# A four-layer attention and feed-forward network on one core: the query and key columns of three attentions are put in another order in memory

## The reference, cut to what matters

```python
q = _heads(x @ Wq + bq)            # (b, 16 heads, 512, 16)
k = _heads(src @ Wk + bk)          # src is x (causal) or the context
v = _heads(src @ Wv + bv)
att = jnp.einsum('bhqd,bhkd->bhqk', q, k) * scale
y = jnp.einsum('bhqk,bhkd->bhqd', jax.nn.softmax(att, axis=-1), v)
y = y.transpose(0, 2, 1, 3).reshape(x.shape[0], T, C)
return y @ Wp + bp
```

## Time and profile before

| What | Value |
|---|---|
| median of 3 runs | 3605.73 us |
| lowest and highest run | 3598.47, 3623.86 us |
| the profiled execution's own time | 3604.23 us |
| its span in the profile | 3602.4 us |
| PE busy | 2886.6 us, 80% |
| DVE busy | 2034.1 us, 56% |
| ACT busy | 1460.1 us, 41% |
| POOL busy | 1147.6 us, 32% |
| DMA packets | 129751, 198.50 MB |

### The profile page before, as it was taken

One profiled execution on the slowest core, in us unless ns is written; L12 is line 12 of the kernel. 1 busy time (PEld: TensorE's weight loads), 2 busy tenths in 40 slices (PEclk: granted clock), 3 DMA queues, 4 the chain that ended last, 5 costly groups with the idle time before them and its releaser, 6 DMA issues. The chain is left out here.

```text
span 3602.4 us, 44895 instructions
## 1 busy us (share of the span) xinstructions
PE 2886.6 (80%) x16756; PEld 1623.2 (45%) x16756; DVE 2034.1 (56%) x3607; ACT 1460.1 (41%) x1932; POOL 1147.6 (32%) x1007
## 2 busy tenths in 40 slices
PE   5998898758867979999876889877899899688544
PEld 2333333533324534444662344356778778223222
DVE  4545546756635735444784666675453543566588
ACT  1444455415652224444422545432433432256522
POOL 2122222221322215555413668741001010122233
PEclk7688889878987989999986989988999999689766
DMA  6344454034521001111100000000221121555100
GB/s 158 76 100 96 103 117 102 19 73 93 112 61 37 1 21 37 37 40 61 60 7 12 1 1 1 13 12 11 68 72 56 56 65 35 114 109 106 29 15 15
DMA packets 129751, 198.50 MB, mean 55 GB/s; under 512 B 36288, under 2 KB 66496, under 8 KB 129408
## 3 DMA queue, kind: packets, MB, share of 16 engines
q1 hardware_dynamic: 97792, 143.23, 17.3%
q0 software_dynamic: 31744, 52.41, 5.3%
HBM read 130.73 MB, written 64.75 MB: 54 GB/s over the span
## 5 line engine op out<-in xcount | busy, mean ns | idle before, releaser
L2202 DVE TENSOR_REDUCE L_mx<-bank_t 128x2 f32<-128x1024 f32 (+3 forms) x512 | 562.5, 1121 | 481.0 <-PE bank_t L2010 300.9
L2409 ACT ACTIVATE L_P<-bank_t 128x1024 f32<-128x1024 f32 (+2 forms) x512 | 478.1, 945 | 483.8 <-PE bank_t L2024 305.8
L2202 DVE TENSOR_REDUCE L2a_mx<-bank_t 128x2 f32<-128x1024 f32 x256 | 311.4, 1222 | 406.7 <-PE bank_t L1987 406.1
L2409 ACT ACTIVATE L2a_P<-bank_t 128x1024 f32<-128x1024 f32 x256 | 261.6, 1023 | 289.4 <-PE bank_t L1999 289.1
L2024 PE MATMUL bank_t<-L_QS,L_KS 50*128 50x512 f32 (+2 forms) x1024 | 242.5, 477 | 111.6 <-DVE L_mx L2202 81.6
L2010 PE MATMUL bank_t<-L_KS,L_QS 48*128 48x512 f32 (+2 forms) x1024 | 262.0, 514 | 75.2 <-DMA L_QS<-L_spill_q_halves 64.5
L1987 PE MATMUL bank_t<-L2a_QK 32*128 32x512 f32 x1536 | 257.5, 453 | 69.9 <-DVE L2a_mx L2202 34.0
L2055 PE MATMUL bank_o<-L_P,L_V 128*32 128x512 f32 (+3 forms) x2048 | 289.8, 642 | 2.6 <-ACT xn L2416 1.8
L1995 PE MATMUL bank_t<-L2a_QK 32*128 32x512 f32 x1536 | 260.4, 448 | 0.0
L2010 PEld LDWEIGHTS bank_t<-L_KS,L_QS 48*128 48x128 f32 x1024 | 107.9, 209 | 320.5 <-issue 222.2
L1987 PEld LDWEIGHTS bank_t<-L2a_QK 32*128 32x128 f32 x1536 | 138.9, 199 | 234.3 <-issue 106.3
(11 more groups left out here) (432 smaller groups left out, 6059.8 us busy)
## 6 DMA issues: line engine op xcount, KB each, us to landing
L_KS<-L_spill_k_halves SPq DMA_DIRECT2D x174, 128.0 KB, 4.5
L_QS<-L_spill_q_halves SPq DMA_DIRECT2D x174, 128.0 KB, 4.9
L_spill_raw<-xn POOLq DMA_DIRECT2D x64, 256.0 KB, 2.5
L2g_raw<-in_L_ffn_h_blocks SPq DMA_DIRECT2D x32, 512.0 KB, 3.4
L_spill_k_halves<-L_hi SPq DMA_DIRECT2D x32, 256.0 KB, 2.1
L_spill_k_halves<-L_lo SPq DMA_DIRECT2D x32, 256.0 KB, 2.3
L_spill_q_halves<-L_hi SPq DMA_DIRECT2D x32, 256.0 KB, 4.8
L_spill_q_halves<-L_lo SPq DMA_DIRECT2D x32, 256.0 KB, 5.0
```

The costliest lines, as they stand in the source:

```text
L2202: e.tensor_reduce(neg, s.tile[:, :, 0:n_keys], AX.X, ALU.max, negate=True).then_inc(sem(s.done), 1)
L2409: e.activation(s.at.Pr[s.pb][:, :, q0:S], s.tile[:, :, q0:S], ACT.Exp, scale=s.at.scale).then_inc(sem(s.exp), 1)
```

## The change

The columns of `Wq` and `Wk` of the three attentions, and the entries of their biases, are put in another order on the host, before the kernel starts: within each 128 columns, from (slot, part, d) to (part, d, slot). A projected half then has row 64q + 4d + s for part q, column d of the head, slot s. The four slots that one partition of a stack takes are now four neighbouring rows of the stored half, 8 KB in one run. The rearrangement in ReadStack follows. The values' weights and the output's weights stay as they are. The loads of weights keep their shapes and their order.

```diff
@@ L0_xattn (L0_first, L1_weights and L3_xattn likewise)
-            loads = [weight_load(W[n][:, :, :], f"L0_xattn_{n}", KC) for n in W]
-            loads += [weight_load(Wc[n][:, :, :], f"L0_xattn_{n}", 1) for n in Wc]
+            loads = [weight_load(W["Wv"][:, :, :], "L0_xattn_Wv", KC), weight_load(W["Wcq"][:, :, :], "L0_xattn_Wcq_runs", KC)]
+            loads += [weight_load(Wc["Wck"][:, :, :], "L0_xattn_Wck_runs", 1), weight_load(Wc["Wcv"][:, :, :], "L0_xattn_Wcv", 1)]
...
@@ sync_program, ReadStack
                     for r, part in enumerate((0, 0, 1) if s.which == "q" else (0, 1, 0)):
-                        halves = s.spill[part].rearrange("(s q d) n -> q d s n", q=st.q_of, d=D)
+                        halves = s.spill[part].rearrange("(q d s) n -> q d s n", q=st.q_of, d=D)
                         for q in range(st.q_of):
                             row = st.part * q + D * r
                             e.dma_start(stack[row:row + D, s.slots, :].bitcast(F32),
...
@@ layout, on the host
+    for n in ("L0_xattn_Wq", "L0_xattn_Wk", "L0_xattn_Wcq", "L0_xattn_Wck", "L1_xattn_Wq", "L1_xattn_Wk",
+              "L3_xattn_Wq_T", "L3_xattn_Wk_T", "L0_xattn_bq", "L0_xattn_bk", "L0_xattn_bcq", "L0_xattn_bck",
+              "L1_xattn_bq", "L1_xattn_bk"):
+
+        w = a[n].reshape(-1, a[n].shape[-1] // P, 4, 2, 16)
+        a[n + "_runs"] = w.transpose(0, 1, 3, 4, 2).reshape(a[n].shape)
```

More of the change, by code:

```diff
@@ L933, in L0_first @@
             f.bq, f.bp = sb(scope, "L0_bcols", [P, 4, KC]), sb(scope, "L0_bp", [P, C])
-            f.loads = [weight_load(f.W["Wk"][:, :, :], "L0_xattn_Wk", KC), load(f.bq[:, 1, :], dram["L0_xattn_bk_cols"]),
-                       weight_load(f.W["Wq"][:, :, :], "L0_xattn_Wq", KC), load(f.bq[:, 0, :], dram["L0_xattn_bq_cols"])]
+            f.loads = [weight_load(f.W["Wk"][:, :, :], "L0_xattn_Wk_runs", KC), load(f.bq[:, 1, :], dram["L0_xattn_bk_runs_cols"]),
+                       weight_load(f.W["Wq"][:, :, :], "L0_xattn_Wq_runs", KC), load(f.bq[:, 0, :], dram["L0_xattn_bq_runs_cols"])]
             f.e_bp = row_load(f.bp, "L0_xattn_bp")
@@ L954, in L0_xattn @@
                 fetch_x(b)
-            loads = [weight_load(W[n][:, :, :], f"L0_xattn_{n}", KC) for n in W]
-            loads += [weight_load(Wc[n][:, :, :], f"L0_xattn_{n}", 1) for n in Wc]
+            loads = [weight_load(W["Wv"][:, :, :], "L0_xattn_Wv", KC), weight_load(W["Wcq"][:, :, :], "L0_xattn_Wcq_runs", KC)]
+            loads += [weight_load(Wc["Wck"][:, :, :], "L0_xattn_Wck_runs", 1), weight_load(Wc["Wcv"][:, :, :], "L0_xattn_Wcv", 1)]
             loads += [weight_load(Wo[:, :, :], "L0_xattn_Wp", KC)]
-            loads += [load(bq[:, i, :], dram[f"L0_xattn_{n}_cols"]) for i, n in ((2, "bcq"), (3, "bck"))]
+            loads += [load(bq[:, i, :], dram[f"L0_xattn_{n}_runs_cols"]) for i, n in ((2, "bcq"), (3, "bck"))]
             loads += [row_load(rows[n], f"L0_xattn_{n}") for n in rows]
@@ L1164, in fetch @@
             def fetch():
-                w.loads[:] = [weight_load(w.Wq[:, :, :], "L1_xattn_Wq", KC), weight_load(w.Wk[:, :, :], "L1_xattn_Wk", 1),
+                w.loads[:] = [weight_load(w.Wq[:, :, :], "L1_xattn_Wq_runs", KC), weight_load(w.Wk[:, :, :], "L1_xattn_Wk_runs", 1),
                            weight_load(w.Wv[:, :, :], "L1_xattn_Wv", 1), weight_load(w.Wo[:, :, :], "L1_xattn_Wo", KC),
-                           load(w.bq[:, 0, :], dram["L1_xattn_bq_cols"]), load(w.bq[:, 1, :], dram["L1_xattn_bk_cols"]),
+                           load(w.bq[:, 0, :], dram["L1_xattn_bq_runs_cols"]), load(w.bq[:, 1, :], dram["L1_xattn_bk_runs_cols"]),
                            row_load(w.bv, "L1_xattn_bv"), row_load(w.bo, "L1_xattn_bo")]
@@ L1629, in L3_xattn @@
             Wv = sb(scope, "L3_Wv", [P, 1, C])
-            loads = [weight_load(Wq[:, :, :], "L3_xattn_Wq_T", KC), weight_load(Wo[:, :, :], "L3_xattn_Wo_T", KC),
-                     weight_load(Wk[:, :, :], "L3_xattn_Wk_T", 1), weight_load(Wv[:, :, :], "L3_xattn_Wv_T", 1)]
+            loads = [weight_load(Wq[:, :, :], "L3_xattn_Wq_T_runs", KC), weight_load(Wo[:, :, :], "L3_xattn_Wo_T", KC),
+                     weight_load(Wk[:, :, :], "L3_xattn_Wk_T_runs", 1), weight_load(Wv[:, :, :], "L3_xattn_Wv_T", 1)]
             e_ctx = load_context(ahead["context"])
@@ L2673, in cols @@
             a[n + "_cols"] = a[n].reshape(-1, P).T
-    cols("L0_xattn_bq", "L0_xattn_bk", "L0_xattn_bcq", "L0_xattn_bck")
     def flip(*names):
@@ L2683, in layout @@
     a["L2_ffn_w3_blocks"] = a["L2_ffn_w3_w"].T.reshape(KF, P, KC, P)
-    cols("L0_ffn_b1", "L1_ffn_b1", "L1_xattn_bq", "L1_xattn_bk", *(f"L2_ffn_{n}_s" for n in ("w1", "w2", "h1", "h2")))
+    cols("L0_ffn_b1", "L1_ffn_b1", *(f"L2_ffn_{n}_s" for n in ("w1", "w2", "h1", "h2")))
     a["L3_xattn_Wk_T"], a["L3_xattn_Wv_T"] = a["L3_xattn_Wkv"][:C].T, a["L3_xattn_Wkv"][C:].T
+    for n in ("L0_xattn_Wq", "L0_xattn_Wk", "L0_xattn_Wcq", "L0_xattn_Wck", "L1_xattn_Wq", "L1_xattn_Wk",
[3 more added lines that the diff above has]
+        a[n + "_runs"] = w.transpose(0, 1, 3, 4, 2).reshape(a[n].shape)
+    cols(*(f"{n}_runs" for n in ("L0_xattn_bq", "L0_xattn_bk", "L0_xattn_bcq", "L0_xattn_bck", "L1_xattn_bq",
+                                 "L1_xattn_bk")))
     a["L1_ffn_scale"] = a["L1_ffn_scale"].reshape(1, 1)
```

## The result

| | before | after |
|---|---|---|
| median | 3604.64 us (20 runs, 3587.66 to 3627.01) | 3621.61 us (20 runs, 3608.41 to 3650.21) |
| ratio | | 1.0058, 95% interval 1.0039 to 1.0078 |
| span of the profiled execution | 3602.4 us | 3648.4 us |
| mean granted clock of that execution | 0.866 | 0.853 |

The changed kernel is slower, by 0.6%, or some 20 us. The interval of the ratio does not reach 1, so the forecast of a gain of 0 to 9 us was wrong in sign, though the median lies within the range of 3570 to 3630 us.

The account below looks back on a forecast made before the run. PE was taken as the first bound, DMA counting only where PE waits. Eight waits of two groups at 0.2 us, three at 0.3 us, and 0.3 us for maxima give 4.4 us off 3604.2, so 3600 us; range 3570 to 3630.

Parts of the forecast that it names:

- the forecast of a gain of 0 to 9 us: Main forecast for the whole kernel, centred on 3600 us, chance 0.63.
- The stake and the waits: PE's 14 waits for the query stack, 64.5 us; eleven within reach, 40.3 us; with the maxima's waits 88 us at stake.
- slot 0: Reads at an attention's start, three waits of 24.2 us in sum; keep 2 KB runs, priced at nothing.
- the five long ones: Five of the eleven waits for the query stack within reach, 28.7 us in sum.
- Packets and issue: Stack reads: 17,856 fewer packets of 129,751, bytes unchanged; SP's issue of six reads gains 0 us.
- Transfer: Moving a group of six stack reads, 5.7 us: longer packets save 3.5%, or 0.2 us per group.
- The faster one: Rival: the narrow DRAM source limits stack reads, spreading it raises the rate; 3575 us, at the bound 3567; chance 0.25.
- the 164 GB/s of the broadcast: Read of the inverse sums from 16 KB of DRAM into 128 partitions, taken as evidence for the faster rival.
- The slower one: Rival: with 8 KB packets engines change over less often, stack reads fall to 111 GB/s; 41 us more, 3645 us; chance 0.07.
- The rule of the Trainium skill: DMA rate goes with ports reached; partitions 0 to 15 reach four of 16, 104 GB/s; it speaks against the change.
- the group stays at 5.7 us: By the port rule alone, six stack reads take as long as before and the sum is zero.

Follow-up runs that it names:

- a unit's chain: Program of its own: six reads, a 512 KB store, its landing, six reads, their landing; 15.79 us in the old order, 16.50 in the new.
- reads alone: Programs with only rounds of six stack reads, everything else left out; 7.40 us a round in the old order, 7.92 in the changed kernel's.
- the new order in packets of 2 KB: Changed kernel with stored rows 2.5 KB apart instead of 2 KB, so packets are 2 KB again; ratio 1.0022 to the kernel before.
- the target spread: Stack reads into every third of 48 partitions, against the kernel before: old order 0.991, new order 0.9887, old order with the queries' store ahead 0.9912.
- the store ahead: Kernel before with the keys' reads issued one tick later, behind the store of the queries' halves; ratio 1.010.

## Why the prediction was wrong

*The stake and the waits* were read rightly. 14 waits, 11 of them within reach and slot 0 outside it: after the change nearly the same waits are there (15), those of slot 0 and the five long ones about the same in sum (23.5 and 28.5 us), most of the short ones longer, 67.6 us in all against 64.5.

*Packets and issue* came out to the number: 17,856 packets fewer, 2.7 us to issue six reads, nothing gained there.

*Transfer* is the step that failed. I took 36 ns of 1032 ns off a partition's 8 KB, 0.2 us per group, from the 12 ns of a packet that do not grow with its bytes. Measured, a group alone is 0.5 us longer (7.92 against 7.40 us), and a unit's chain of two groups 0.7 us longer. No run shows a price of the short packets that could be given back: from SBUF, 2 and 8 KB differ by 0.1 us in 9. And the new layout has a price, which I had not put into the sum at all. With reads alone it goes with the place: rows 10 KB apart instead of 2.5 cost 0.5 us per group with the same packets of 2 KB. I named the place once, for slot 0 ("rows 8 KB apart in DRAM"), and set it to nothing there; it is 0.13 us for its twelve reads. The same distance holds for all the other reads.

*Which property of the layout costs the time in the whole kernel stays open.* There the new order in packets of 2 KB had the old rate and the old landings (143 GB/s; 4.3 and 4.8 us) and ran 14 us faster than the changed kernel, which points to the runs of 8 KB; the reads alone point to the place. Runs of 8 KB cannot stand 2 KB apart, so the two cannot be parted in full, and no run tells why they come out differently. Shown is that the new layout as a whole makes a group slower.

*The rivals.* The faster one looked to the source, with the sign wrong: I read the 164 GB/s of the broadcast as "a narrow source is slow", when a source spread wider is what turned out slower. The slower one had the sign (a rate of 115 to 131 GB/s in place of 137) and its price, 41 us, was for 111 GB/s. Its cause, long packets into two narrow targets in turn, is not borne out by the reads alone, but it is not ruled out either: in the whole kernel the loss went when the packets were cut to 2 KB, and it was not seen with the target spread.

*The rule of the Trainium skill* that I weighed, "SBUF — State Buffer", section "Door 1: The DMA port swizzle (why [64,N] ≈ [32,N])", by which 16 neighbouring partitions are the limit, is borne out: every third of 48 partitions took a round from 7.27 to 6.19 us and the kernel down by 0.9%. The rule says nothing on a distance at the source, and "the group stays at 5.7 us" was what I drew from it; as long as the target is narrow, the layout at the source still adds to it.

*The size.* 7.7 us are worked out from the chains, 10 us are measured at an equal clock, 17 to 27 us in the medians. The remaining part goes with a granted clock that is 0.004 lower. The direction is the same in the other runs (0.870 to 0.873 for the three kernels with the target spread, 0.862 for the one with the store ahead and the target narrow), so I take it that more standing still of PE brings more time at 1.2 GHz; that is argued from the mean clocks of these kernels, not shown by taking the clock apart from the waits.

*What stays open* besides: why a greater distance between the rows in DRAM slows reads alone; why the new order in 2 KB packets is slower alone but not in the whole kernel; and why, with the target spread, the two orders take the same time.

## What to carry to other kernels

Before packets are made longer, ask whether they are what is short: here the same 2 KB packets ran at 397 GB/s into DRAM and at 137 GB/s into 16 neighbouring partitions. The target was the limit, and spreading it (three interleaved groups in place of three blocks) took 0.9%, with a change of two lines that costs PE nothing (its scores take 510 ns each on average, 514 before). Where rows are put in a new order to make runs longer, look also at how far apart the rows for neighbouring partitions come to stand, not only at what one partition reads. Where a transfer can be timed in a program of its own, time it there: half a microsecond is clear in seven, and hard to see in 3600. But test the cause in the whole kernel too, against the changed kernel itself: here the two programs did not agree on it.

## What the runs showed of the hardware that I had not expected

Six reads of 128 KB from DRAM into 16 partitions took 7.3, 7.75, 7.9 and 8.3 us as the rows of neighbouring partitions stood 2, 4, 8 and 16 KB apart (at 8 KB in one run of 8 KB per partition, in the others in runs of 2 KB). From SBUF (16 partitions to 16 partitions) the same took 9.0 us, slower than from DRAM. A read into every third partition takes SP 0.63 us to issue, one into neighbours 0.45.
